# A convolution kernel's last sample: its mix in the middle of the preceding convolution, its relay on two queues, its interleaving on three engines

## What is computed

```python
x = x + conv0(x)    # grouped convolution, 4 groups of 32 channels, 9 taps, plus a bias from the condition
x = x + mix1(x)     # 1x1 convolution; its 128x128 matrix is a softmax-weighted sum of 8 matrices, per sample
x = x + mix2(x)     # the same again with other weights
x = x + conv3(x)    # grouped convolution as the first
```

## Time and profile before

| | |
|---|---|
| median of three runs | 726.29 us (725.65 to 726.70) |
| the profiled execution's own time | 726.53 us |
| its span, from the first to the last instruction | 724.7 us |
| TensorE busy | 676.0 us, 93% of the span |
| VectorE, ScalarE, GpSimd busy | 457.9, 256.5, 253.9 us |

### The profile page before, as it was taken

One profiled execution on the slowest core, in us unless ns is written; L12 is line 12 of the kernel. 1 busy time (PEld: TensorE's weight loads), 2 busy tenths in 40 slices (PEclk: granted clock), 3 DMA queues, 4 the chain that ended last, 5 costly groups with the idle time before them and its releaser, 6 DMA issues.

```text
span 724.7 us, 24030 instructions
## 1 busy us (share of the span) xinstructions
PE 676.0 (93%) x10924; PEld 568.1 (78%) x10924; DVE 457.9 (63%) x909; ACT 256.5 (35%) x319; POOL 253.9 (35%) x94
## 2 busy tenths in 40 slices
PE   4847999999999999999999999999999999999970
PEld 3645888888888888888888888888888888888860
DVE  5378667666666666766666666767676766675321
ACT  3312433344334443334433444333433344332311
POOL 7022243333334444334333444433433444422220
PEclk9956999999999999999999999999999999999996
DMA  8131478789988888888998788888898878666657
GB/s 268 62 88 44 107 186 184 182 165 183 202 160 183 188 189 185 189 180 153 195 184 178 180 188 188 182 192 174 156 203 180 174 182 191 132 130 132 108 91 168
DMA packets 50237, 119.72 MB, mean 165 GB/s; under 512 B 5864, under 2 KB 25368, under 8 KB 42264
## 3 DMA queue, kind: packets, MB, share of 16 engines
q1 hardware_dynamic: 48592, 118.66, 74.9%
q10 hardware_dynamic: 1352, 0.57, 0.3%
q0 software_dynamic: 256, 0.01, 0.0%
HBM read 35.33 MB, written 33.55 MB: 95 GB/s over the span
## 4 chain that ended last, share of the span: by engine, by line
PE 91%; DVE 3%; DMA 2%; ACT 1%; ACTq 1%; issue 0%; SPq 0%; DVEq 0%
PE ps L676 76%; PE ps L712 12%; PE ps L700 2%; DMA out_planes<-out_taps 1%; DMA out_sb<-in_fside_S 1%; DVE out_planes L554 1%; DVE acc L537 1%; PE ps L741 1%; DVE y_lo L500 0%; DVE z_lo L510 0%; DVE x_lo L493 0%; DVE mat2T L537 0%; ACT out_sb L408 0%; PE ps L766 0%; DVE mat L537 0%
## 5 line engine op out<-in xcount | busy, mean ns | idle before, releaser
L334 POOL COPY out_sb<-out_planes 128x2048 f32<-128x2048 f32 x31 | 122.6, 3956 | 315.1 <-DMA out_planes<-out_taps 315.1
L327 POOL COPY x_planes<-x_in 128x2048 f32<-128x2048 f32 x31 | 120.3, 3881 | 135.8 <-DVE x_lo L493 132.2
L676 PE MATMUL ps<-z_hi,taps_hi 32*128 32x512 f32 x1536 | 160.2, 401 | 3.7 <-DVE z_lo L510 3.7
L676 PE MATMUL ps<-x_hi,taps_hi 32*128 32x512 f32 x1536 | 159.4, 396 | 0.7 <-DVE prod L547 0.7
L676 PE MATMUL ps<-x_lo,taps_hi 32*128 32x512 f32 x1536 | 158.2, 393 | 0.0
L676 PE MATMUL ps<-x_hi,taps_lo 32*128 32x512 f32 x1536 | 158.0, 393 | 0.0
L676 PE MATMUL ps<-z_hi,taps_lo 32*128 32x512 f32 x1536 | 157.7, 393 | 0.0
L676 PE MATMUL ps<-z_lo,taps_hi 32*128 32x512 f32 x1536 | 157.2, 392 | 0.1
L385 ACT ACTIVATE y_hi<-ps,bias_tab 128x512 fp32r<-128x512 f32 x128 | 77.6, 690 | 211.5 <-PE ps L676 211.5
L510 DVE SCALAR_TENSOR_TENSOR z_lo<-ps,bias_tab,z_hi 128x1024 fp32r<-128x1024 f32 x64 | 79.2, 1279 | 75.2 <-ACT z_hi L395 75.2
L500 DVE SCALAR_TENSOR_TENSOR y_lo<-ps,bias_tab,y_hi 128x512 fp32r<-128x512 f32 x128 | 87.3, 744 | 46.7 <-ACT y_hi L385 46.7
(11 more groups left out here) (99 smaller groups left out, 509.7 us busy)
## 6 DMA issues: line engine op xcount, KB each, us to landing
out_planes<-out_taps SPq DMA_DIRECT2D x128, 256.0 KB, 7.0
x_in<-in_x SPq DMA_DIRECT2D x31, 1024.0 KB, 10.2
out<-out_sb SPq DMA_DIRECT2D x31, 1024.0 KB, 4.2
mix_w<-prod SPq DMA_DIRECT2D x128, 128.0 KB, 4.5
x_in<-in_x SPq DMA_DIRECT2D x2, 512.0 KB, 6.4
out<-out_sb SPq DMA_DIRECT2D x2, 512.0 KB, 3.1
out_taps<-in_L_cond_weight SPq DMA_DIRECT2D x1, 512.0 KB, 9.6
mix_w<-in_L_cond_weight SPq DMA_DIRECT2D x1, 512.0 KB, 13.2
```

Source lines behind the costliest of these rows:

```text
L327: pool.tensor_copy(x_planes[:, :, :], x_in[t.par(d)][:, :].rearrange("c (s p) -> c p s", p=PH))\
L334: pool.tensor_copy(out_sb[t.par(d)][:, :].rearrange("c (s p) -> c p s", p=PH), out_planes[:, :, :])\
L676: tile = pe.matmul(ps[:, first_bank + g, :], w[rows(g), d, :], a[rows(g), d % PH, d // PH:d // PH + S], start=(n == 0), stop=(n == TURNS - 1))
```

## The change

Four things are changed, all for samples 30 and 31:

1. In step 31 TensorE runs `mix` of sample 31 between the two halves of `conv3` of sample 30, and no longer behind it.
2. z of sample 31 is written to `x_hi[0]` and `x_lo[0]`, which no sample needs any more (`z_last`, `z_home`), since `conv3` of sample 30 still reads `z_hi` and `z_lo`. ScalarE and VectorE make this z ahead of `evac_out` of sample 30 and no longer behind it.
3. The four relays of sample 31 are issued by SyncE (groups 0 and 2) and by ScalarE (groups 1 and 3).
4. The interleaving of sample 31 is split in three: VectorE makes the first half, ScalarE the third quarter, GpSimd the fourth. SyncE stores the first half, ScalarE the second.

```diff
+        z_last = (x_hi[N % 2], x_lo[N % 2])
+        def z_home(t, d):
+            return z_last if t.at(N - 1 - d) else (z_hi, z_lo)
+        LAST_WEAVE = (slice(0, S // 2), slice(S // 2, 3 * S // 4), slice(3 * S // 4, S))
+        def weave_last(q):
+            s = LAST_WEAVE[q]
+            return (out_sb[1][:, PH * s.start:PH * s.stop].rearrange("c (s p) -> c p s", p=PH), out_planes[:, :, s])
+        def relay_last(eng, g):
+            eng.dma_start(out_planes[rows(g), :, :], out_taps[:, g, :]).then_inc(last_relaid[g], DMA)
...
@@ sync
-            for g in range(G):
-                if g < 2:
-                    sp.wait_ge(out_act, 2 * b + g + 1)
-                else:
-                    sp.wait_ge(out_dve, 2 * b + g - 1)
-                if g == 0:
-                    sp.wait_ge(out_woven, b)
-                sp.dma_start(out_planes[rows(g), :, :], out_taps[:, g, :])\
-                  .then_inc(last_relaid[g], DMA)
-            for h in range(2):
-                sp.wait_ge(last_woven[h], 1)
-                sp.dma_start(out[b, :, h * L // 2:(h + 1) * L // 2], out_sb[b % 2][:, h * L // 2:(h + 1) * L // 2])\
-                  .then_inc(out_stored[b % 2], DMA)
+            sp.wait_ge(out_woven, b)
+            sp.wait_ge(out_act, 2 * b + 1)
+            relay_last(sp, 0)
+            sp.wait_ge(out_dve, 2 * b + 1)
+            relay_last(sp, 2)
+            sp.wait_ge(last_woven[0], 1)
+            sp.dma_start(out[b, :, 0:L // 2], out_sb[b % 2][:, 0:L // 2]).then_inc(out_stored[b % 2], DMA)
...
@@ gpsimd
+            for g in range(G):
+                pool.wait_ge(last_relaid[g], DMA)
+            pool.wait_ge(out_stored[1], DMA * (N // 2 - 1))
+            o, i = weave_last(2)
+            pool.tensor_copy(o, i).then_inc(last_woven[2], 1)
...
@@ scalar (the order in one(t) of vector is changed in the same way)
-                if t.has(-1):
+                if t.at(N - 1):
+                    high_z(t)
                     evac_out(t, -1)
-                if t.has(0):
+                elif t.has(-1):
+                    evac_out(t, -1)
+                if t.has(0) and not t.at(N - 1):
                     high_z(t)
...
+            act.wait_ge(out_woven, N - 1)
+            act.wait_ge(out_act, 2 * N)
+            relay_last(act, 1)
+            act.wait_ge(out_dve, 2 * N)
+            relay_last(act, 3)
             for g in range(G):
                 act.wait_ge(last_relaid[g], DMA)
             act.wait_ge(out_stored[1], DMA * (N // 2 - 1))
-            weave_last(0)
+            o, i = weave_last(1)
+            act.activation(o, i, ACT.Copy).then_inc(last_woven[1], 1)
+            act.wait_ge(last_woven[1], 1)
+            act.wait_ge(last_woven[2], 1)
+            act.dma_start(out[N - 1, :, L // 2:L], out_sb[1][:, L // 2:L]).then_inc(out_stored[1], DMA)
...
@@ tensor
+                if t.at(N - 1):
+                    mix(t)
                 if t.has(-1):
                     conv3(t, -1, range(MID, TURNS))
-                if t.has(0):
+                if t.has(0) and not t.at(N - 1):
                     mix(t)
```

More of the change, by code:

```diff
@@ L193, in conditioned_residual_kernel @@
         last_relaid = [sem(f"last_relaid{g}") for g in range(G)]
-        last_woven = [sem(f"last_woven{h}") for h in range(2)]
+        last_woven = [sem(f"last_woven{q}") for q in range(3)]
         out_stored = [sem(f"out_stored{i}") for i in range(2)]
@@ L394, in high_z @@
                     k = bank(t, 0) + 2 * h
-                    act.activation(z_hi[:, 2 * h:2 * h + 2, 1:S + 1], ps[:, k:k + 2, :], ACT.Identity,
+                    act.activation(z_home(t, 0)[0][:, 2 * h:2 * h + 2, 1:S + 1], ps[:, k:k + 2, :], ACT.Identity,
                                    bias=bias_tab[:, b, 2 * G:BIAS]).then_inc(z_hi_done, 1)
@@ L404, in evac_out @@
                                    bias=bias_tab[:, b, G + g:G + g + 1]).then_inc(out_act, 1)
[L406 to L409, removed]
             def taps_high(l, p):
@@ L509, in low_z @@
                     k = bank(t, 0) + 2 * h
-                    dve.scalar_tensor_tensor(out=z_lo[:, 2 * h:2 * h + 2, 1:S + 1], in0=ps[:, k:k + 2, :],
+                    dve.scalar_tensor_tensor(out=z_home(t, 0)[1][:, 2 * h:2 * h + 2, 1:S + 1], in0=ps[:, k:k + 2, :],
                                              scalar=bias_tab[:, b, 2 * G:BIAS],
-                                             in1=z_hi[:, 2 * h:2 * h + 2, 1:S + 1].bitcast(F32),
+                                             in1=z_home(t, 0)[0][:, 2 * h:2 * h + 2, 1:S + 1].bitcast(F32),
                                              op0=ALU.add, op1=ALU.subtract).then_inc(z_lo_done, 1)
@@ L580, in one @@
                     low_x(t, 2)
-                if t.has(-1):
+                if t.at(N - 1):
+                    low_z(t)
                     evac_out(t, -1)
-                if t.has(0):
+                elif t.has(-1):
+                    evac_out(t, -1)
+                if t.has(0) and not t.at(N - 1):
                     low_z(t)
@@ L664, in _ @@
             dve.wait_ge(out_stored[1], DMA * (N // 2 - 1))
-            dve.tensor_copy(out_sb[1][:, L // 2:L].rearrange("c (s p) -> c p s", p=PH), out_planes[:, :, S // 2:S])\
-               .then_inc(last_woven[1], 1)
+            o, i = weave_last(0)
+            dve.tensor_copy(o, i).then_inc(last_woven[0], 1)
         @block.tensor
@@ L692, in conv3 @@
                     pe.wait_ge(z_lo_done, 2 * (b + 1))
-                conv_turns(bank(t, d), 1, z_hi, z_lo, conv3_done, turns)
+                conv_turns(bank(t, d), 1, *z_home(t, d), conv3_done, turns)
             def product(t, d):
```

## The result

The changed kernel takes 727.80 us (median of 13 runs, 727.26 to 728.59), the kernel before 725.73 us in the same sessions (13 runs, 725.15 to 726.70). The ratio is 1.0028, with a 95% interval of 1.0020 to 1.0037: slower by 2.0 us. The forecast was 725.1 us and slightly faster; the time lies inside the stated range, but it moved the other way. The profiled execution took 728.50 us for a span of 726.7 us, where the serial rival had said 728.2 and 726.6.

What follows compares the result with a forecast made beforehand. TensorE was busy 93% of the span, but a second chain through sample 30's relays and interleaving decided: +2.79, -3.08 and -0.90 make -1.2 us, span end 723.5, median 725.1 us; range 723.8 to 728.4.

Steps and rivals of the forecast that it cites:

- the serial rival: Store and sample 31's relays: engines serve both rings in line, 12.37 us stay; end 726.6, time 728.2 us; chance 0.26.
- TensorE's part: Steps 31 and 32: mix fits without a wait, clock stays up, sample 31's conv3 ends at 700.9, 5.8 us earlier.
- the second chain: Sample 30's conv3 end, relays, interleaving and store, which hold sample 31's relays back: all 2.79 us later.
- the engines take from both rings in turn: Sample 30's store and sample 31's relays: transfers of two queues mix, 9.29 us in place of 12.37; chance 0.62.
- the term of -3.08: From sample 30's store issue to sample 31's last landing: 9.29 us in place of 12.37.
- hold each other up no more: Relays of groups 0 and 3 together, into different partitions: 2.8 us for the pair, between 1.25 and 4.3.
- The argument against the serial rival: Relays' fast first stretch, 244 GB/s, taken to show that reading is not what is slow.
- four times 2.15 and 0.4 at the ends: Split of the 9.0 us from 709.0 to sample 31's last landing: 2.15 us per relay group.
- The forecast's own sign for mixing: DMA windows from 709.3 to 712.4 stay near 400 GB/s; near 120 from the start would make the prediction wrong.
- the last term: Sample 31's interleaving in three: landing to span end 5.76 us where it was 6.66, 0.9 us gained.
- that case: GpSimd's quarter held up by VectorE's copy: 1.08 us late, covered by the first half's store, no cost.

Runs made afterwards that it cites:

- The mix alone: Against the kernel before: only sample 31's mix moved between sample 30's conv3 halves, z in idle x buffers; relays and interleaving as before; 1.0036, 2.6 us slower.
- the kernels with own buffers: Changed kernel, sample 31 evacuated into an idle input buffer, relayed into x_planes, sample 30's store after the relays: 0.9907; mix unmoved 1.0003, then one queue 0.9982; moved, one queue 0.9914.
- the two queues alone: Against the kernel before: only sample 31's four relays issued from SyncE and ScalarE, mix and interleaving as before; 0.9994.
- the kernel with the store behind: Changed kernel with sample 30's store issued after SyncE's two last relays instead of ahead of them; 0.9992 to the kernel before.
- The interleaving alone: Against the kernel before: only sample 31's interleaving split in three and its two stores issued from two queues; 0.9982, 1.3 us faster.

## Why the prediction was wrong

**Right: TensorE's part.** The mix began at 685.45 (685.52 forecast), no wait for y_lo or z, `conv3` of sample 31 from 692.47 (692.49), the clock at 1.00. That the starts agree to a tenth is luck, since those of single executions differ by more; the lengths between them are what was right. **Right: the second chain.** Relays of sample 30 from 694.29 (694.31), interleaving from 704.72 (704.58), store issued at 708.58 (708.46). The mix alone cost 2.6 us (2.79 by the sum). The prediction's reason, that `out_planes` and `out_taps` and not TensorE hold sample 31 back, is shown by the kernels with own buffers, where the moved mix is worth 4.9 us on one queue (7.0 on two) after costing 2.6.

**Wrong: "the engines take from both rings in turn, store and group 1 share the first stretch ... then groups 0 and 3 together".** It was to give back 3.08 us (9.29 in place of 12.37); the measured stretch is 12.40, and the two queues alone give 0.9994. What the runs show in its place is one line for both queues: transfers pass one after the other in the order in which their issues ended, with little overlap, so the term of -3.08 was +0.03. This is the serial rival, which had 0.26. That pieces going into different partitions "hold each other up no more" was given the middle of its bounds, 2.8 us for a pair; the one pair of relays that passed side by side for long, in the kernel with the store behind, went at 126 and then 184 GB/s, and in the changed kernel no pair did.

The argument against the serial rival, that the relays begin fast, was misread. The fast start is not spare room for a second queue but belongs to the first relay behind a store or a pause: 238 GB/s in the changed kernel, nearly all of it from ScalarE's queue, and 244 on one queue before. Where the relays of sample 31 come directly behind those of sample 30, with own buffers, there is none (window 702 to 703 us):

```profile
702.00:703.00 1.00, 0.00 (x0) 0.00 (x0) 0.00 (x0) 0.00 (x0) 0.00 (x0) 1.00 1.04 129
```

The pieces of the 9.0 us were misread with it: "four times 2.15 and 0.4 at the ends" has the right sum, but by the earlier trace rows 244 GB/s for 1.0 us and 123 for 6.5 have moved nearly all of the 1.05 MB by 716.5. The landing at 718.04 came over 1 us later than that, and the first relay took about half of 2.15. The DMA share of 1 at 123 GB/s was the row to go by. The forecast's own sign for mixing, some 400 GB/s from 709.3 to 712.4, could not have told the cases apart: the store alone gives 389 up to 712.0.

The Trainium skill's "DMA: Bandwidth & Descriptors", section "Issuing engines are not separate DMA queues", which says that a second issuing engine saves only the time of issuing, agrees with this case's 0.9994, and the case should have had the largest chance. The same page of the Trainium skill, section "Queues, rings and completion order", says that an engine goes round the queues that have work and drains a whole packet of one before it turns to the next. The round is not seen here: in the kernel with only the relays changed to two queues, two of SyncE's pass before the first of ScalarE's, which had been issued 1.6 us before the first one's last bytes (708.21 and 709.85).

**The size of the last term.** Landing to end took 5.7 us (5.76 forecast). GpSimd's quarter took 2.02 us and not 1.0, and as the prediction had it for that case it cost little or nothing: the second store was issued 1.0 us after the first and its bytes follow the first half's. The interleaving alone gave 1.3 us (0.9 forecast, 0.7 to 2.0 by the interval).

**The sum as it was:** +2.79 for the second chain, 0 for the queues, -0.9 to -1.3 for the interleaving, +1.5 to +1.9; measured +2.0. From the measured parts it is +2.6 and -1.5, +1.1; their intervals of about 1 us each cover the difference.

## What to carry to other kernels

Before work is moved to close a gap on the busiest engine, follow the chain that runs beside it and ask what the move does to that: here a wait of 3.7 us was closed by delaying the sample before by 2.8 us, and that sample held the buffers which the last one needed. Free those buffers first (idle ones were at hand), and the same move is worth about 5 us. In this case's DMA stretch, with a share of 1 at 123 GB/s, a second queue added nothing. Look instead at what the transfers look like, and at what stands ahead of them in line, over both queues: a store that nobody waits for, issued just ahead of relays on the critical chain, cost 2 us or more, and one issued 0.3 us ahead of the last relay cost 1.5.

## What the runs showed of the hardware that was not expected

- By one execution each, copies of 128 pieces of 2 KB from SBUF to SBUF pass at 341 GB/s into their own 128 partitions, at 254 when the halves change places, at 196 from 32 partitions into the same 32, at 126 from 128 partitions into 32 and at 117 into 16.
- Transfers of 128 pieces on the two queues pass in the order in which their issues ended, not in turns between the queues; two of SyncE's passed in a row while one of ScalarE's stood issued. In one kernel this put 1 MB ahead of the last relay and cost 1.5 us.
- A relay of 256 KB that comes behind a store or a pause passes in about 1.1 us; one directly behind another relay takes 2.1. Why is not shown.
- A copy of 128x1024 fp32 on VectorE, of 1.08 to 1.10 us, stops a GpSimd copy beside it for nearly its whole length (2.02 against 1.09 us).
- Issuing the same relay on SyncE took 0.55 to 0.61 us where the first came 1.7 us after the store's issue (2.50 for four, before), and up to 1.38 where it came 0.4 us after it (3.77 for four, with the mix alone); the last landing was no later for it, 12.37 us after the store's issue in both.
